# Half of each batch's base products behind the next scan transposes, and the second normalisation measured on ScalarE

## What is computed

```python
x = x + tanh(g_xattn[0]) * mamba0(ctx_1024, layernorm(x))
x = x + tanh(g_ffn[0])   * moe(layernorm(x))            # 16 experts, 4 per token, and a shared one
x = x + tanh(g_xattn[1]) * mamba1(ctx_1024, layernorm(x))
x = x + tanh(g_ffn[1])   * lora_moe(layernorm(x))
```

```python
result = x @ base_w.T + base_b
probs = softmax(x @ router_w.T + router_b); top 2, renormalised -> gate
mid = (x @ lora_A) * gate                    # (tokens, 8, 16)
return result + 2.0 * mid @ lora_B
```

## Time and profile before

| | before |
|---|---|
| runs, us | 1515.09, 1518.84, 1520.01 |
| the profiled execution, us | 1520.53 |
| its span, us | 1518.8 |
| TensorE matmuls, busy us (share) | 1271.5 (84%) |
| VectorE, busy us (share) | 1384.6 (91%) |
| ScalarE, busy us (share) | 871.9 (57%) |
| GpSimd, busy us (share) | 788.0 (52%) |
| chain that ended last, largest shares | VectorE 35%, TensorE 30%, issue 8%, DMA 6% |

### The profile page before, as it was taken

How to read it: one execution, slowest core, us unless ns; L and a number is a source line. 1 busy time by engine, 2 the same in 40 slices (tenths; PEclk the granted TensorE clock), 3 DMA queues, 4 the chain that set the end, 5 groups by cost and what they waited for, 6 DMA issues and landing times.

```text
span 1518.8 us, 14557 instructions
## 1 busy us (share of the span) xinstructions
PE 1271.5 (84%) x4518; PEld 725.1 (48%) x4518; DVE 1384.6 (91%) x1413; ACT 871.9 (57%) x1448; POOL 788.0 (52%) x411
## 2 busy tenths in 40 slices
PE   7785796898699868986989998899988889836998
PEld 3331332443244324442556666566665666625555
DVE  4999999898989899988899999999899999988894
ACT  5866567575865675625865755546655444424442
POOL 0465566445544553540465556654565666555642
PEclk9898899899989998998999999999999999977999
DMA  7344456535544554450466678677787888755531
GB/s 257 102 145 128 116 151 142 139 97 150 137 134 123 126 126 109 125 152 2 101 183 228 235 253 296 230 257 236 244 275 232 272 259 284 255 190 145 167 103 56
DMA packets 99836, 264.30 MB, mean 174 GB/s; under 512 B 10832, under 2 KB 11344, under 8 KB 93616
## 3 DMA queue, kind: packets, MB, share of 16 engines
q1 hardware_dynamic: 87936, 225.36, 50.7%
q0 software_dynamic: 11440, 37.50, 7.4%
q10 hardware_dynamic: 384, 0.52, 0.1%
HBM read 233.73 MB, written 29.62 MB: 173 GB/s over the span
## 4 chain that ended last, share of the span: by engine, by line
DVE 35%; PE 30%; issue 8%; DMA 6%; POOL 5%; ACT 3%; DVEq 0%; SPq 0%; another core or an unknown queue 0%; ACTq 0%; POOLq 0%
DVE state L1706 15%; DVE banks L1698 10%; PE banks L1182 8%; PE banks L1092 5%; PE banks L1193 3%; DMA expert_w<-in_moe_w 3%; PE banks L1141 2%; DVE y_scan L1717 2%; POOL state L457 2%; PE banks L1036 2%; PE banks L1149 2%; DMA ys_d<-expert_out 1%; PE banks L1013 1%; DVE du L1424 1%; DVE hidden L1724 1%
## 5 line engine op out<-in xcount | busy, mean ns | idle before, releaser
L457 POOL TENSOR_TENSOR state<-state,bc_rows 128x1024 f32<-128x1024 f32 x254 | 599.1, 2359 | 628.2 <-DVE banks L1698 628.0
L1092 PE MATMUL banks<-state,ident 128*128 128x512 f32 x640 | 328.3, 645 | 107.9 <-POOL state L457 107.6
L1706 DVE TENSOR_TENSOR_SCAN state<-decay,banks 128x1024 f32<-128x1024 f32 x176 | 402.1, 2285 | 10.2 <-ACT decay L712 5.8
L1698 DVE TENSOR_TENSOR banks<-du,bc_rows 128x1024 f32<-128x1024 f32 x256 | 314.6, 1229 | 13.4 <-DVE state L1706 0.5
L1182 PE MATMUL banks<-z_gate,expert_w 128*128 128x256 f32 (+1 forms) x1504 | 284.1, 347 | 6.8 <-DMA expert_w<-in_moe_w 6.7
L1182 PEld LDWEIGHTS banks<-z_gate,expert_w 128*128 128x128 f32 x1504 | 249.0, 191 | 59.7 <-issue 20.7
L712 ACT ACTIVATE decay<-delta,neg_a 128x511 f32<-128x511 f32 x352 | 230.5, 712 | 48.5 <-DVE state L1706 43.7
L1092 PEld LDWEIGHTS banks<-state,ident 128*128 128x128 f32 x640 | 119.1, 199 | 284.0 <-POOL state L457 171.0
L1706 DVE TENSOR_TENSOR_SCAN state<-expert_w,banks 128x1024 f32<-128x1024 f32 x80 | 182.9, 2286 | 8.3 <-ACT expert_w L712 5.7
L1193 PE MATMUL banks<-expert_w,hidden 128*128 128x512 f32 x316 | 155.6, 608 | 2.9 <-DVE hidden L1727 2.9
L1717 DVE TENSOR_TENSOR y_scan<-y_scan,state 128x1024 f32<-128x1024 f32 x94 | 114.0, 1212 | 3.6 <-POOL state L457 3.6
(11 more groups left out here) (318 smaller groups left out, 1647.7 us busy)
## 6 DMA issues: line engine op xcount, KB each, us to landing
bc_rows<-bc_d SPq DMA_DIRECT2D x208, 512.0 KB, 5.0
expert_w<-in_moe_w SPq DMA_DIRECT2D x48, 1536.0 KB, 9.2
ys_d<-expert_out SPq DMA_DIRECT2D x32, 512.0 KB, 10.2
ctx_t<-in_ctxT SPq DMA_DIRECT2D x8, 512.0 KB, 6.6
x_res<-in_x SPq DMA_DIRECT2D x4, 1024.0 KB, 10.8
xn_d<-y_scan SPq DMA_DIRECT2D x4, 1024.0 KB, 7.6
ys_d<-expert_out SPq DMA_DIRECT2D x15, 256.0 KB, 9.5
out_x<-x_res SPq DMA_DIRECT2D x3, 1024.0 KB, 6.0
```

What stands on the lines that cost most here:

```text
L457: nc.gpsimd.tensor_tensor(W[:, c % 4], W[:, c % 4], bcast2(BC[:, u, 1, :]), ALU.mult).then_inc(mulc_done, 1)
L1092: mm = nc.tensor.matmul(PS[:, m], ID[:, :], W[:, c % 4, m, :], start=False, stop=True, skip_group_check=True)
L1698: nc.vector.tensor_tensor(drive(s), DU[:, s % 2, 2 * h:2 * h + 2, :], bcast2(BC[:, u, 0, :]), ALU.mult).then_inc(mulb_done, 1)
L1706: nc.vector.tensor_tensor_scan(flat(W[:, c % 4]), flat(DAS[c % da_slots(s, i)]), flat(drive(s)), 0.0, ALU.mult, ALU.add).then_inc(scan_don ...
```

## The change

TensorE, for b from 1 to 3, issues base(l, 0) and base(l, 1), then the scan transposes, then the transposes of MID, then base(l, 2) and base(l, 3), then LoRA B. The warming products of these iterations go from 14 to 4. In the last iteration (b = 4), which has no scan transposes, all four base products stay together.

ScalarE gets `deviations(f)` in place of `rstd_root(2f + 1)`: a Sqrt of a single column, which brings the table load ahead of the wait for the scan's additions; the mean from sums that these additions now accumulate (ROWSUM); four Squares of x less its mean, each with an accumulated sum (into SQ); and the Sqrt of the variance. VectorE no longer runs the second `tail_stats`. Instead it takes the reciprocal of that root in `norm_bias`. Two more combines of the next batch stand ahead of `norm_bias`, and `lora_add(l)` moves from the end of iteration b into iteration b + 1, behind the combines up to the fourteenth. The last one stands behind the loop.

```diff
@@ ScalarE
+            def deviations(f):
+                nc.scalar.activation(SQ[:, 0, 0:1], EPSC[:, :], ACT.Sqrt)
+                act.wait_ge(xacc, QT * (f + 1))
+                nc.scalar.activation(NMEAN[:, 1, :], ROWSUM[:, 1, :], ACT.Copy, scale=-1.0 / D).then_inc(tail_mean, 1)
+                act.wait_ge(tail_mean, f - NB + 1)
+                for q in range(QT):
+                    ins = nc.scalar.activation(ZS[:, q, :], X[:, f % NB * QT + q, :], ACT.Square,
+                                               bias=NMEAN[:, 1, q:q + 1], accum_out=SQ[:, 1, q:q + 1])
+                ins.then_inc(var_ready, 1)
+                act.wait_ge(var_ready, 2 * f + 2)
+                nc.scalar.activation(RS[:, :], SQ[:, 1, :], ACT.Sqrt, scale=1.0 / D, bias=EPSC[:, :]).then_inc(std_ready, 1)
...
                 if b < NB:
-                    rstd_root(2 * f + 1)
+                    deviations(f)
                     act.wait_ge(zn_ready, 2 * f + 2)
@@ TensorE
                     base(l, 0)
                     base(l, 1)
-                    base(l, 2)
-                    base(l, 3)
-                    pe.wait_ge(midg_ready, l + 1)
-                    for q in range(QT):
-                        mm = nc.tensor.transpose(PRE[1][:, q * P:(q + 1) * P], MID[:, q, :], ID[:, :])
-                    mm.then_inc(midt_done, 1)
+                    if b == NB:
+                        base(l, 2)
+                        base(l, 3)
                 if b == 0:
                     pe.wait_ge(rows_zn, 1)
                     stay_warm(PRE[1], 24)
...
                     y_transposes(f, Y[:, b], (0, 1))
                     y_transposes(f, Y[:, b], (2, 3))
                 if l >= 0:
+                    pe.wait_ge(midg_ready, l + 1)
+                    for q in range(QT):
+                        mm = nc.tensor.transpose(PRE[1][:, q * P:(q + 1) * P], MID[:, q, :], ID[:, :])
+                    mm.then_inc(midt_done, 1)
+                    if b < NB:
+                        base(l, 2)
+                        base(l, 3)
                     pe.wait_ge(midt_ready, l + 1)
...
                 if b < NB:
-                    stay_warm(PRE[1], 14)
+                    stay_warm(PRE[1], 4 if b else 14)
@@ VectorE
-                    total = None if gate else ROWSUM[:, 1, lt:lt + 1]
                     nc.vector.scalar_tensor_tensor(out=xr, in0=AUX[lt % 2], scalar=TG[:, gate:gate + 1], in1=xr, op0=ALU.mult,
-                                                   op1=ALU.add, accum_out=total).then_inc(xacc, 1)
+                                                   op1=ALU.add, accum_out=ROWSUM[:, 1, lt:lt + 1]).then_inc(xacc, 1)
...
                 dve.wait_ge(std_ready, v + 1)
-                if v < 2 * NB:
+                if v >= 2 * NB and v % 2:
+                    link(nc.vector.reciprocal(RS[:, :], RS[:, :]))
+                if v < 2 * NB or v % 2:
                     nc.vector.tensor_tensor(NBI[:, :], NMEAN[:, v % 2, :], RS[:, :], ALU.mult).then_inc(zn_ready, 1)
...
                 if 0 < b < NB:
-                    combine(b, QT, TOPK * QT)
+                    combine(b, QT + 2, TOPK * QT - 2)
+                if b >= 2:
+                    lora_add(b - 2)
+                if 0 < b < NB:
+                    combine(b, TOPK * QT - 2, TOPK * QT)
...
                     scan_add(f, range(QT), 1)
-                    dve.wait_ge(xacc, QT * (f + 1))
-                    tail_stats(b)
                     if b + 1 < NB:
-                        combine(b + 1, 2, QT)
+                        combine(b + 1, 2, QT + 2)
                     norm_bias(2 * f + 1)
-                if l >= 0:
-                    lora_add(l)
+            lora_add(NB - 1)
```

More of the change, by code:

```diff
@@ L209, in build @@
         hg_ready, y_done, yev, dve_step = sem("hg_ready"), sem("y_done"), sem("yev"), sem("dve_step")
+        tail_mean = sem("tail_mean")
         rows_var, rows_std, rows_zn, rows_z = sem("rows_var"), sem("rows_std"), sem("rows_zn"), sem("rows_z")
```

## The result

The changed kernel takes 1529.61 us (median of 6 runs, 1525.6 to 1535.94), the kernel before, run beside it, 1515.38 (6 runs, 1514.14 to 1520.01). The ratio is 1.0084, 95% interval 1.0060 to 1.0109: slower, inside the range and 2.6 us above the forecast. The profiled execution of the changed kernel took 1529.58 us with a span of 1527.9, against 1520.53 and 1518.8. That is 9.1 us more where the sum said 8.1.

The account below looks back on a forecast made before the run. TensorE and VectorE are both nearly full in the tail's batches, so order within a batch decides. Three batches cost 8.9 us more, less 0.8 from batch 0: plus 8.1 on the median 1518.84 gives 1527 us, range 1518 to 1533.

Parts of the forecast that it names:

- The pause: Before the scan transposes: half of base covers 6.87 of 11.0 us to the gating, so TensorE idles 4.1 us per batch.
- faster: Rival, chance 0.10: in the tail the gating comes sooner than 11 us, as VectorE's queue is 3.3 us shorter; 1516.2 us.
- nothing: Rival, chance 0.05: in the tail TensorE's pause and the shorter warming cancel; 1519 us.
- Everything late: Rival, chance 0.09: in the tail gathers land in 5.0 us and the clock costs 2.35 us each time; 1531.3 us.
- From the gating to the next M: Tail, gating's end (Y) to the batch's last router product (M): 21.65, 21.65 and 21.20 us, plus 0.05 hand-over.
- The clock: TensorE's clock falls to 0.5 behind each pause of about 4.1 us, slowing the scan transposes by 1.0, 1.0 and 1.5 us.
- the harmless rival: Rival, chance 0.14: in the tail the clock holds and the gather is not late; plus 1.9, 1520.7 us.
- The gathers: Fourth row block's gather lands 2.8 us after its last issue; next logits 35.35, then 36.4 us after the preceding router products end.
- ScalarE's measurement: Second normalisation: three rows done 12.2 us behind the gating, TensorE asks at 15.0; nothing on the path, 2.8 us of cover.
- combines moved: same count, they lie in VectorE's wait: Two more combines before the norm's product, two fewer later, within VectorE's wait for ScalarE; no cost.
- Batch 0: First tail batch, without base products: the norm starts at 1388.8 instead of 1389.58, 0.8 us gained, 2 us uncertain either way.
- Shorter warming: Ahead of the row transposes: 2.23 us fewer warming products per batch, giving back less than the lost cover's 4.1 us.

Follow-up runs that it names:

- e2: Kernel before with only the split: base products in two halves, MID transposes behind the scan's, 14 warming products; 1529.69 us, ratio 1.0098.
- e3: Changed kernel with 17 warming products between the first half of base and the scan transposes; 1526.83 us, ratio 1.0051.
- e1: Changed kernel with all four base products and MID's transposes back ahead of the scan transposes; 1523.35 us, ratio 1.0044.
- e7: Kernel before with 4 warming products instead of 14 in iterations 1 to 3; 1516.61 us (one run).
- k5: Kernel before with the stores of batches 0 and 1 held until the last gathers of batches 2 and 3 landed; 1512.03 us (one run).
- k2: Kernel before with ScalarE's measurement and 4 warming products, first two combines ahead of the norm's product; 1517.80 us, ratio 1.0007.
- e5: Changed kernel with the last gathers issued ahead of GpSimd's bias addition; 1529.04 us, ratio 1.0070.
- k1: Kernel before with ScalarE's measurement and 4 warming products, first two combines behind the norm's product; 1512.29 us, ratio 0.9988.
- k7: k1 with 12 warming products instead of 4; three batch distances sum to 95.83 us, whole time not given.
- k3: e1 without GpSimd's bias addition, so the base bias is left out of the output; 1509.79 us (one run).
- k4: k7 with the stores of batches 0 and 1 held until the last gathers of batches 2 and 3 landed; 1516.94 us, ratio 0.9985.

## Why the prediction was right, by its own steps

**The pause.** Right in kind and size: 4.18 us forecast 4.1 for the first; 5.40 and 5.18 where 4.1 plus the wait for late logits (1.55 and 1.06) are 5.65 and 5.16. Nothing shortened logits to gating (10.96, 11.16, 10.94), so the rival "faster" fell, and "nothing" with it; e2 shows that the split alone does it. "Everything late" fell on the landing of the gathers (2.6, not 5.0).

**From the gating to the next M.** Without the clock 21.7, 21.7 and 21.25 were worked out, and e3 measured 21.87, 21.87 and 21.26.

**The clock.** That it would fall was right each time, so the harmless rival fell. Its price was mis-sized by batch: 1.0, 1.0 and 1.5 forecast, 1.95, 0.76 and 0.96 measured, 3.5 and 3.67 in sum. What differs is how long the low clock lasted behind the gating: 6.6, 4.2 and 3.4 us. In the first batch it lasted beyond the transposes, into MID's (1.06 for 0.60) and base (7.90 for 7.03), which the step hadn't priced. In the third the block of sixteen lasted 3.80 us and not 4.3, without the hand-overs that I had added. In the first the terms can be read beside e3's: transposes 4.15 for 3.45 us from first start to last end, MID 0.46, base 0.87, together 2.03. By the Trainium skill's half of the throttled time (TensorE: Matmul & The Clock Gate, section "HAM oscillation — how this bites in real kernels") 6.6, 4.2 and 3.4 us at the low clock would be 3.3, 2.1 and 1.7, an estimate; the two executions show 1.95, 0.76 and 0.96. At full clock e3's transposes waited 1.12 us for VectorE between their two groups, and at the low one 0.24: that wait took up part of the loss.

**The gathers.** The landing was right (1431.49 - 1428.87 = 2.6, forecast 2.8), and so were the 6.05 us from it to the logits (6.08). The end of the last issue was M0 + 27.67 instead of M0 + 26.5: the step took GpSimd's chain of before as it was. With combines beside them, three of its issues now take 1.43, 1.23 and 1.29 us instead of 0.95, and the addition starts 0.44 later. Hence logits at M0 + 36.37, not 35.35; but M1 was late by 1.1 too, so that their distance from M1 (1.55) is near the forecast (35.35 - 33.7 = 1.65). The next logits were forecast at M1 + 36.4 and came at M1 + 36.40. That exactness is luck: the last issue ended 0.3 later than forecast (M1 + 27.80) and its gather landed 0.3 sooner (2.5).

**ScalarE's measurement.** Right in its result, with two terms wrong. The MIDT copy starts at Y + 5.1, not Y + 3.9, as the transposes ahead of it run at the low clock. And "combines moved: same count, they lie in VectorE's wait" missed GpSimd's addition, which holds them until 1423.24 and the norms until Y + 12.6 instead of Y + 9.9. TensorE was late as well (it asked at Y + 16.9, not 15.0), so 2.1 us of cover were left, and 1.2 in the next batch. In e1, where TensorE isn't late, the same hold cost it a wait of 4.34 us. The trace of before had hinted at it, in VectorE's timeline and in GpSimd's:

```profile
1422.19 1.06 DVE L1927 TENSOR_SCALAR rstd<-mean_var 128x4 f32<-128x4 f32 x1
```
```profile
1418.67 4.53 POOL L504 TENSOR_TENSOR x_res<-x_res,softplus_tmp 128x2048 f32<-128x2048 f32 x1
```

An instruction on four columns, 0.17 us elsewhere, took 1.06 and ended 0.05 after the addition. I had not asked why. In e2 the same instruction took 2.66 and 2.84.

**Batch 0.** Forecast 0.8 gained. Its norms started at 1388.73 instead of 1389.58, as worked out, but M0 came only 0.4 sooner, and even that isn't shown to be the change's doing: from the end of its gating to M0 the changed kernel took 20.81 us, and the four kernels with an unchanged batch 0 (before, e2, e7, k5) took 21.12, 21.24, 19.15 and 21.24. **Shorter warming** "gives back less": true here, but the 2.23 us are no gain by themselves (e7).

**The total.** Distances 33.7, 35.35, 34.8 forecast, 34.82, 35.34, 34.23 measured: 103.85 and 104.39. In the profiled pair 9.1 us against 8.1. The ratio of all runs says 1.0084 x 1515.4 - 1515.4 = 12.7 us. Some 3.5 us of that are not in the tail's distances; the profiled execution of before was one of its slowest, and M0's own wandering between executions is as large. What makes M0 wander was not tried and stays open. That the time itself was met within 2.6 us is in part luck: the forecast stood on a median of three runs (1518.84), and the six of the result have 1515.38. From there the same sum gives 1523.5, which is 6.1 below what was measured. The mechanism and its size in the tail were forecast (8.9 against 9.46); the whole difference was forecast a third too small.

## What to carry to other kernels

Work that stands in front of a wait isn't in the way of what waits: here 13.7 us of products covered 11 us of VectorE's work, and moving half of them behind uncovered it without making anything earlier. Before moving such work, ask what ends last at that wait, and look whether the clock fell behind pauses of that length elsewhere in the same trace. When combines or the like (two inputs in SBUF) are moved on VectorE, look at what GpSimd does at that moment: here one addition of 4.5 us on its queue held a combine until it ended.

## What the runs showed of the hardware that I hadn't expected

- GpSimd's addition of 128x2048 (4.54 us) held one VectorE combine for 4.58, 4.87 and 5.21 us instead of 0.74 (e1, k2, e5), and a `tensor_scalar` on four columns for 1.06 and 0.82 (before), 2.66 and 2.84 (e2) and 2.06 us (k5) instead of 0.17. The reverse is there too: a gather's issue that meets the gating (two inputs in SBUF) takes 2.79 us instead of 0.95.
- A gather of the last row block landed 5.0 to 6.5 us after its last issue with a store of 1 MB under way (before, e7, k1, k2, k7), and 2.5 to 3.1 without (changed kernel, e1, e3, k3, k4, k5).
- Waits of 1.74 to 4.34 us ahead of the row transposes, behind only 1.05 us of warming products, were followed by a granted clock of 0.50 in e1, e7, k1 and k2. Of the waits of 1.37 and 1.38, those in e1, k1 and k2 and two in k3 were not, and one in k3 was, so that the length of the wait alone doesn't decide here. With 2.84 us of warming (k4) the waits were 0 to 0.64, and the clock stayed at 1.00 through all three batches; with 3.29 us (k5) it fell behind a wait of 1.80.
- Two costs of this kind replace each other: in k1 and k2, e1 and e7 what a shorter wait gained was lost or regained by the moment at which the clock fell, so that a single change of 1 to 3 us in this tail can't be read from one distance alone.
